# A layer of attention and routed experts: expert tiles of 256 rows instead of 512, in two phases, with the weights split beforehand

## The reference

```python
mod = (silu(c) @ wmod).reshape(4, 6, 1, 256)        # sa, ca, ga, sb, cb, gb per batch
ga, gb = sign * max(|.|, 0.25) of each              # gates kept away from zero
h = layernorm(x) * (1 + ca) + sa                    # x: 4 x 2048 x 256
q, k, v = h @ W_qkv                                 # 16 heads of 16
x = x + ga * (softmax(causal(q k^T) / 4) v) @ W_o
h = layernorm(x) * (1 + cb) + sb
probs = sigmoid(h @ router_w.T);  topw, sel = top_k(probs, 2);  topw /= sum(topw)
out = sum over the 2 chosen e of  topw_e * relu(h @ w1_e)**2 @ w2_e
x = x + gb * out
```

## Time and profile before

| what | value |
|---|---|
| three runs | 2795.98, 2794.82, 2787.42 us; median 2794.82 |
| profiled execution | 2796.0 us span; the run of 2795.98, with nothing around it |
| TensorE matmul busy | 2529.9 us, 90% |
| VectorE, ScalarE, POOL busy | 2179.1, 1727.6, 692.7 us |
| DMA | 331.82 MB, mean 119 GB/s |

### The profile page before, as it was taken

The page is one execution under the profiler, slowest core; times in us unless marked ns, Lnnn a source line. Parts: engine busy times, 40 slices in busy tenths (PEclk is TensorE's granted clock), DMA queues, the critical chain, the costliest instruction groups (busy, mean ns, idle before and its releaser), DMA issues. The chain is left out here.

```text
span 2796.0 us, 49392 instructions
## 1 busy us (share of the span) xinstructions
PE 2529.9 (90%) x16192; PEld 1298.9 (46%) x16192; DVE 2179.1 (78%) x5287; ACT 1727.6 (62%) x3481; POOL 692.7 (25%) x721
## 2 busy tenths in 40 slices
PE   7978999999999999999999999999996579999990
PEld 6852333333333333333333333333332479999990
DVE  6979889888888788888888898888821867777761
ACT  4640576777666666666666667666674257777760
POOL 3453333000010101011010110101012435556553
PEclk9986899999999999999999999999998689999995
DMA  6989788412404234040431404234012635555548
GB/s 213 316 280 301 275 282 286 145 27 57 97 28 97 56 73 116 13 117 29 96 92 37 120 22 104 52 78 105 16 54 84 217 84 92 88 90 91 91 68 255
DMA packets 218336, 331.82 MB, mean 119 GB/s; under 512 B 27408, under 2 KB 158224, under 8 KB 218096
## 3 DMA queue, kind: packets, MB, share of 16 engines
q1 hardware_dynamic: 137728, 170.48, 21.4%
q0 software_dynamic: 58704, 136.86, 19.7%
q10 hardware_dynamic: 21664, 21.50, 2.5%
HBM read 140.75 MB, written 187.20 MB: 117 GB/s over the span
## 5 line engine op out<-in xcount | busy, mean ns | idle before, releaser
L1007 ACT ACTIVATE probs<-ps 128x512 f32<-128x512 f32 (+3 forms) x2400 | 1122.2, 539 | 587.5 <-PE ps L1335 339.4
L1033 DVE TENSOR_REDUCE early<-ps 128x1 f32<-128x512 f32 x1536 | 1001.5, 684 | 106.0 <-PE ps L1240 100.1
L1240 PE MATMUL ps<-kh,qs 96*128 96x512 bf16 (+3 forms) x2560 | 882.2, 361 | 88.0 <-DVE early L1033 37.4
L1335 PE MATMUL ps<-qs,kh 99*128 99x512 bf16 (+3 forms) x2560 | 831.1, 352 | 17.0 <-ACT probs L1007 6.6
L1351 PE MATMUL ps<-probs,vs 128*32 128x512 f32 (+3 forms) x5120 | 605.8, 545 | 0.0
L1240 PEld LDWEIGHTS ps<-kh,qs 96*128 96x128 bf16 x2560 | 250.7, 99 | 700.5 <-DVE early L1033 303.6
L1029 DVE CUSTOM_DVE_ANT_0 junk<-ps,causal 128x128 bf16<-128x128 f32 (+3 forms) x1024 | 480.7, 483 | 52.8 <-PE ps L1240 48.0
L1335 PEld LDWEIGHTS ps<-qs,kh 99*128 99x128 bf16 x2560 | 246.1, 98 | 290.7 <-ACT probs L1007 135.8
L1760 POOL DMA_INDIRECT acc<-y,to x156 | 250.6, 1606 | 119.0 <-ACT y L1815 73.9
L926 POOL DMA_INDIRECT rows_out<-row,place_a x96 | 95.2, 991 | 698.5 <-DVE place_a L697 650.8
L1339 PE MATMUL ps<-ident_b,causal_b 128*128 128x128 bf16 x1024 | 214.0, 221 | 0.0
(11 more groups left out here) (231 smaller groups left out, 3011.2 us busy)
## 6 DMA issues: line engine op xcount, KB each, us to landing
rows_out<-row POOLq DMA_DIRECT2D x129, 544.0 KB, 3.6
xg<-rows_out SPq DMA_DIRECT2D x39, 544.0 KB
v_ones<-vt SPq DMA_DIRECT2D x16, 1024.0 KB, 6.4
vs<-v_ones SPq DMA_DIRECT2D x16, 1024.0 KB, 11.2
contexts<-ctx_out SPq DMA_DIRECT2D x64, 256.0 KB
q_parts<-parts SPq DMA_DIRECT2D x32, 384.0 KB, 4.6
k_parts<-parts SPq DMA_DIRECT2D x32, 384.0 KB, 4.6
qs<-q_parts SPq DMA_DIRECT2D x64, 192.0 KB, 7.3
```

The lines of the kernel that those rows point to most:

```text
L1007: nc.scalar.activation(probs[u % PB][:, h, q0:TB], bank(s % SB)[:, q0:TB], ACT.Exp, scale=SCALE).then_inc(exp_done, 1)
L1033: nc.vector.tensor_reduce(early[:, h, t, k0 // CW:k0 // CW + 1], tile, AX.X, ALU.max).then_inc(max_done, 1)
L1240: nc.tensor.matmul(tile[:, 0:w], qh[a % HR][0:STACK, t * P:(t + 1) * P], kh[a % HR][0:STACK, k0:k0 + w], start=True, stop=True).then_inc(m ...
L1335: mm = nc.tensor.matmul(tile[:, q0:TB], kh[a % HR][:, kt * P:(kt + 1) * P], qh[a % HR][:, j * TB + q0:(j + 1) * TB], start=True, stop=not ...
```

## The change

Tiles have 256 rows (`RT` = 2 subtiles). There are 71: the first 41 (`FULL`) take only full tiles of the rows that the 12 hidden blocks have sent; their table is computed first. The four late blocks are routed inside the same block of instructions, at fixed steps `BASE[m] + L_...` of the slice counter q, by the same engines between the expert work; SP fetches and stores for them (`fetch`, `store_over`), POOL sends their rows between its adds. After step 130 a second table gives the last 30 tiles (`LATE`). The weights are split once, in the prologue of `attend` (ScalarE high part, POOL rest), and go to DRAM; all of w2 is loaded back and stays, its slice chosen by a register on TensorE; of w1 each tile gets its 1 MB by DMA. `dispatch_rest` is gone. The adds take the token number straight from the gathered rows; six buffers for rows, three for results.

```diff
+FULL = -(-(2 * HIDDEN_BLOCKS * TB - E * (TR - 1)) // TR)      # 41
+LATE = (2 * T - FULL * TR + E * (TR - 1)) // TR               # 30
+UP_AHEAD, UP_SLOTS = 2, 3
+HB = 6
+XG = 6
+WB = 3
+YB = 3
+PIECES = 6
+BASE = [1 + PITCH * m for m in range(LATE_BLOCKS)]            # PITCH = 32
+FETCH_AT = [0] + [(b + 24) // FW + 4 for b in BASE[:-1]]
+OVER_AT = [(b + 22) // FW + 3 for b in BASE]
...
# attend, ScalarE, ahead of the first group
+                load_piece(0)
+                load_piece(1)
+                for n in range(PIECES):
+                    act.wait_ge(raw_in[n % 2], 16 * (n // 2 + 1))
+                    nc.scalar.activation(staged(n, 0).bitcast(F32R), staged(n, None), ACT.Copy).then_inc(w_high, 1)
+                    act.wait_ge(w_high, n + 1)
+                    act.dma_start(weight_piece(n, 0), staged(n, 0)).then_inc(parts_out, 16)
+                    act.wait_ge(w_low, n + 1)
+                    act.dma_start(weight_piece(n, 1), staged(n, 1)).then_inc(parts_out, 16)
+                    if n + 2 < PIECES:
+                        load_piece(n + 2)          # from n = 2 on it waits for parts_out, 32 * (n - 1)
# attend, POOL, ahead of the fills; attend, SP, in group 2: w2_hi <- w2_parts[0]
+                for n in range(PIECES):
+                    pool.wait_ge(w_high, n + 1)
+                    nc.gpsimd.tensor_tensor(staged(n, 1).bitcast(F32R), staged(n, None), staged(n, 0), ALU.subtract
+                                            ).then_inc(w_low, 1)
...
# experts, SP
+                def gather(i):
+                    if i == FULL:
+                        sp.wait_ge(table_steps, BOTH_TABLES)
+                        sp.wait_ge(sent, 128 * LATE_BLOCKS)
+                    ...
+                    if i >= XG:
+                        sp.wait_ge(g_mm, i - XG + 1)
+                        sp.wait_ge(y_done, RT * (i - XG + 1))
+                        sp.wait_ge(added, 16 * RT * (i - XG + 1))
+                def weights(i):
+                    ...
+                    if i >= WB:
+                        sp.wait_ge(u_mm, FW * (i - WB + 1))
+                    for n in range(2):
+                        sp.dma_start(w1_of[i % WB][:, :, n, :].bitcast(F32), w1_parts[n, :, bass.ds(first, W)].rearrange(
+                            "(k p) c -> p k c", p=P)).then_inc(w1_in[i % WB], 16)
+                for i in range(2, NT):
+                    if i in FETCH_AT:
+                        fetch(FETCH_AT.index(i))
+                    if i in OVER_AT:
+                        store_over(OVER_AT.index(i))
+                    gather(i)
+                    if i >= WB:
+                        weights(i - 1)
# experts, POOL
+                def add(i):
+                    pool.wait_ge(y_done, RT * (i + 1))
+                    if i:
+                        pool.wait_ge(added, 16 * RT * i)
+                    if i == FULL:
+                        pool.wait_ge(over_out, 16 * LATE_BLOCKS)
+                    for t in range(RT):
+                        nc.gpsimd.indirect_dma_start(acc[:, :], ..., y[i % YB][:, t, :], None, compute_op=ALU.add
+                                                     ).then_inc(added, 16)
# experts, ScalarE (weigh waits, from i = YB on, for added of tile i - YB)
+                for q in range(NQ):
+                    rectify(q)
+                    if q:
+                        high_hidden(q - 1)
+                    if f == 0 and i and i + 1 < NT:
+                        high_rows(i + 1)
+                    if f == FW - 1 and i:
+                        weigh(i - 1)
+                    ...                              # root, turned, router_exp of the late blocks
# experts, VectorE
+                    square(q)
+                    if q:
+                        low_part(q - 1)
+                    if f == 1 and i and i + 1 < NT:
+                        low_rows(i + 1)
+                    for m in range(LATE_BLOCKS):
+                        late(m, q - STEP_LAG - BASE[m])
# experts, TensorE (transposes(i) waits for g_hi and g_lo of tile i - 1)
+                    if f == 0:
+                        pe.reg_load(slab, tiles[0:1, i, 1:2])
+                        at["slice"] = pe.snap(slab, min_val=0, max_val=NW - FW)
+                    for t in range(RT):
+                        w_hi, w_lo = (w[:, bass.ds(at["slice"] + f, 1), :].squeeze(1) for w in (w2_hi, w2_lo))
+                        nc.tensor.matmul(o, hi, w_hi, ...)
+                        nc.tensor.matmul(o, hi, w_lo, ...)
+                        mm = nc.tensor.matmul(o, lo, w_hi, ...)
...
+                for q in range(NQ):
+                    if f == 1 and i + 2 < NT:
+                        transposes(i + 2)
+                    if q + UP_AHEAD < NQ:
+                        up(q + UP_AHEAD)
+                    if q:
+                        down(q - 1)
+                    ...                              # project, late_transposes, route, count
-def dispatch_rest(...):                             # whole function
```

More of the change, by code:

```diff
@@ L1401, in sb @@
             return sb_(name, shape, dt, own)
-        blocks = range(NBLK - HIDDEN_BLOCKS)
-        sums = sb("sums_r", [P, H * TB // P])
[L1405 to L1412, removed]
+        w1_of = [sb(f"w1_of{k}", [P, KK, 2, W], F32R) for k in range(WB)]
+        w2_lo = sb("w2_lo", [P, NW, D], F32R)
+        xg = [sb(f"xg{k}", [P, RT, ROW]) for k in range(XG)]
+        h_hi = [sb(f"h_hi{p}", [P, KK, TR], F32R) for p in range(2)]
+        h_lo = [sb(f"h_lo{p}", [P, KK, TR], F32R) for p in range(2)]
+        relu = [sb(f"relu{k}", [P, TR]) for k in range(HB)]
+        hid = [sb(f"hid{k}", [P, TR]) for k in range(HB)]
+        hid_hi = [sb(f"hid_hi{k}", [P, TR], F32R) for k in range(HB)]
+        hid_lo = [sb(f"hid_lo{k}", [P, TR], F32R) for k in range(HB)]
+        y = [sb(f"y{k}", [P, RT, D]) for k in range(YB)]
+        tiles = sb("tiles", [P, NT, 4], I32)
+        wide = sb("wide", [P, NT])
+        tile_i = sb("tile_i", [P, FULL], I32)
+        tile_f = sb("tile_f", [P, FULL])
+        need_i = sb("need_i", [P, E], I32)
+        need = sb("need", [P, E])
+        ends = sb("ends", [P, E])
+        taken = sb("taken", [P, E])
+        shift = sb("shift", [P, E])
+        table = sb("table", [P, E, E])
+        past = sb("past", [P, FULL, E])
+        behind = sb("behind", [P, FULL, E])
+        which = sb("which", [P, FULL])
+        start = sb("start", [P, FULL])
+        source = sb("source", [P, FULL])
+        slices = sb("slices", [P, FULL])
+        work = [sb(f"late{k}", [P, KK * TB]) for k in range(4)]
+        num, den, h2t = (w[:, :].rearrange("p (k t) -> p k t", k=KK) for w in work[0:3])
+        centred, over, gated, xres = (w[:, :].rearrange("p (t d) -> p t d", t=TT) for w in work)
+        sums = sb("sums_r", [P, H * TB // P])
+        row = [sb(f"row{p}", [P, TT, ROW]) for p in range(2)]
         stats = sb("stats_r", [P, TT, 6])
@@ new lines, in _ @@
+                for m in range(2):
+                    name_tokens(m)
+                for i in range(NT):
+                    add(i)
+                    for m in range(LATE_BLOCKS):
+                        done = SENDS[m] * (i - SEND_FROM[m])
+                        if 0 <= done < 2 * TT:
+                            for part in range(done, done + SENDS[m]):
+                                send(m, part)
+                        if m >= 2 and i == SEND_FROM[m] - 2:
+                            name_tokens(m)
@@ L1543, in residual, with low_rows @@
[L1543 to L1551 removed]
+                def low_rows(i):
+                    if i >= 2:
+                        dve.wait_ge(u_mm, FW * (i - 1))
+                    dve.wait_ge(g_hi, i + 1)
+                    nc.vector.tensor_tensor(h_lo[i % 2][:, :, :], rows_t(),
+                                            h_hi[i % 2][:, :, :].bitcast(F32), ALU.subtract).then_inc(g_lo, 1)
@@ L1589, in choose @@
[L1589 to L1597 removed]
+                    ts = slice(2 * half, 2 * half + 2)
@@ L1902, in _ @@
+                taken_tiles()
                 for q in range(NQ):
```

856 lines of the change are left out of this document (403 added, 453 removed).

## The result

The changed kernel takes **2883.42 us** (median of four runs, 2881.45 to 2892.0) against 2792.28 of the kernel before beside it: ratio 1.0337, 95% interval 1.0316 to 1.0358, slower by 91 us where 48 less were forecast. The profiled run took 2883.54 us, its span is 2881.8.

What follows compares the result with a forecast made beforehand. TensorE was taken to bound the expert stage, with exposed routing for 107 us ahead of it. Terms -91 +2 -37 +31 +16 +10 +19 -2 +4 gave -48: 2796.0 to 2748, as median 2747 us; range 2696 to 2800.

Steps and rivals of the forecast that it cites:

- POOL and the DMA engines, +19: Expert stage: adds' chain 6.5 us, transfers 6.3 to 6.8 per tile; 6.8 taken in the 30 last tiles, +19 us.
- the adds carry the stage: Rival, POOL's wait for landings in every tile: w1 transfers stretch landings to 4.65, tile 8.2 us, total 2817; chance 0.14.
- The dispatch stage, -89: Ahead of the experts: exposed routing goes, first up matmul about 2162 against 2252.8, -91, with +2 for cold start.
- +2 for cold pipelines: Start of the expert stage: starting with cold pipelines costs 2 us.
- Pace, -37: TensorE in the expert stage: 71 tiles of 6.17 us, 438 instead of 474.8 us, nearly all from less padding.
- the prediction's own sign (0.16 or more): Spacing of down matmul starts on TensorE: 0.119 us expected to stay; 0.16 or more would show the sequencer rival.
- the sequencer rival: TensorE's down matmuls: register operations of 0.046 us for w2's address show, up to 99 us, total 2827; chance 0.10.
- Late blocks on TensorE, +31: Expert stage: projection, transposes, routing and counting of four late blocks add 7.8 us each to TensorE, 31 us.
- Late steps, +16: Expert chain beside late blocks: table loads, compare and share step on ScalarE and VectorE delay TensorE about 4 us per block.
- SP's queue, +10: SP's in-order issue: store_over waits for over_gate, delaying gather and weights 2.5 to 3 us once per block, 10 us.
- Tail, -2: A term of -2 us in the prediction's sum; the text given does not derive it.
- Prologue, +4: Prologue: 2 MB of raw weights requested while TensorE waits for the first head's keys, +4 us, between 0 and 6.

Runs made afterwards that it cites:

- the last version with two accumulators: Changed kernel with w1 unsplit in SBUF, first four gathers issued earlier, w2 alone split in the prologue, odd tiles adding into a second tensor: 2756.17 us.
- w1 kept raw: Changed kernel with w1 unsplit in SBUF, ScalarE and VectorE making its high and low parts per tile instead of DMA copies: 2760.38 us.
- the run with two accumulators: Changed kernel with odd tiles adding into a second tensor, summed in the output stage, all w1 traffic kept: 2785.72 us.

## Why the prediction was wrong

**The step that failed is POOL and the DMA engines, +19.** It had the right chain, 1.61 + 0.3 + 1.61 + landing, and the right 6.3 us of transfer per tile. It took the landing at 2.95, as in the earlier trace rows, read beside a queue at 15.5%, for a stage in which that queue would be at 49%. It then compared two sums, 6.5 for the chain and 6.8 for the engines, and took the larger, as if they ran side by side. They do not: the chain contains the time in which the engines move the adds' packets, and these run late beside the copy. Measured, the median landing is 5.7 and a tile takes 9.1 to 9.4; the prediction's own chain gives 3.52 + 5.72 = 9.2 with that landing. And it priced only the last 30 tiles, since 6.8 would not show below 7.6. At 9.37 it showed in the first 41 too: (9.37 - 7.6) x 41 + (9.06 - 6.17) x 30 = 73 + 87 = 160 in place of 19. Removing only the traffic brought the landing back to 2.96 and 142 us; removing only the wait brought 98 us, after the output stage's cost; adding only traffic to the kernel before cost it 51 us.

The rival *the adds carry the stage* had this mechanism, its place and the point from which it decides (7.9 us per tile), and named the outcome's direction. It got 0.14 and 2817, because it stretched the landing to 4.65. The reason against it, that landings are steady at 2.9 to 3.0 while the DMA engines are half busy, was read from a stage without large copies. Whether copies and adds meet now and then or in every tile was not asked: SP's gather waits for the very landing that starts the next adds, so they meet tile after tile.

**The other steps, by the trace.**

- *The dispatch stage, -89*: measured -91 from the last p_v group to the first up matmul, which ran at 2158.2 (forecast 2162). But "+2 for cold pipelines" was too small: TensorE waits 9.9 us for the third tile's rows and is busy 12.1 of the 22 us after 2158, behind 5 MB or more requested at once.
- *Pace, -37*: 6.23 us against 6.17. The down matmuls stay 0.12 apart in the changed kernel, with their operand addressed through a register:

```profile
2571.46 0.28 PE L1991 MATMUL ps<-w_lo,hid_hi 128*128 x1
2571.58 0.28 PE L1992 MATMUL ps<-w_hi,hid_lo 128*128 x1
2571.70 0.28 PE L1990 MATMUL ps<-w_hi,hid_hi 128*128 x1
2571.82 0.28 PE L1991 MATMUL ps<-w_lo,hid_hi 128*128 x1
```

  By the prediction's own sign (0.16 or more) the sequencer rival falls, and a tile at 6.23 us leaves no room for it. Its 0.046 us was read from ScalarE's rows, not TensorE's.
- *Late blocks on TensorE, +31*: in the last version with two accumulators TensorE is busy 261.9 of the 280 us after 2200, in which 148 row transposes, 37 tiles, are recorded: 7.08 a tile, so (7.08 - 6.17) x 41 = 37: the forecast was slightly low.
- *Late steps, +16*: leaving out the eight table loads brought 2.6, within the spread, in the version with w1 kept raw. The chain that had no slack on paper has some; that it comes from the buffers was not shown.
- *SP's queue, +10*: lies within the larger stall; not isolated.
- *Tail, -2*: +6; the last add starts 16 us after the last matmul where it was 12.
- *Prologue, +4*: TensorE's wait for the first keys grew from 16.4 to 20.4, and the first exponential came at 300.5 instead of 296.7, as forecast. But attention still ended 4 us earlier, 8 us shorter from there; that is not explained, and it is about what runs of one kernel differ by.

With w1 kept raw the stage takes 515.8 us; the prediction's terms for it sum to 474.8 - 37 + 31 + 16 + 10 + 19 = 514. Some of that is luck: +16 was too high, the cold start and the late blocks too low. The changed kernel's stage takes 649.7, 136 us more than that sum, and the total was missed by 136 as well. So what was missed is what the w1 traffic does to the stage. By the run with two accumulators some 117 of the 145 us that this traffic costs the stage come through the wait for landings; the other 28 or so are the copies' in some other way that no run isolates.

## What to carry to other kernels

A wait for a DMA to land is not a constant: read it beside the traffic that the change will bring, and when a chain contains such a wait, price it again with the new copies ahead of it. Spare DMA bandwidth did not mean short landings here: with the same 1 MB per tile the engines were 68% busy and the tile took 9.1 us, or 96% busy at 6.3, depending only on whether a landing stood in the chain. Ask too what wakes the queue that issues the copies; if it is the event that also starts the latency-bound transfer, the two can collide every time.

## What the runs showed of the hardware

- The landing of a pair of indirect adds (256 rows of 1 KB) is 2.9 to 3.0 us alone, 3.8 beside 512 KB, 5.7 to 5.8 beside 1 MB in rows of 1 or 2 KB, 6.4 beside 1 MB in rows of 4 KB. The adds' own packets run late; from the last of them to the next add it is 1.1 us with a copy and without.
- In the changed kernel the adds' last packet comes 0.7 us after the copy's, by medians. While both are under way, 238 rows of 1 KB pass beside 265 copy rows of 2 KB; with copy rows of 1 KB it is 240 beside 774.
- TensorE's granted clock is 0.89 from 2520 to 2660 in the changed kernel, where it is busy 112 of 140 us with a pause in each tile, and 1.00 in the same stretch with two accumulators, where it is busy 139.
